# Causal attention: the probability-times-value products of two blocks issued together, every second block, with a third probability buffer

## The chip, the cores and the metric

One core of a Trainium2 chip runs the whole program in one launch. The metric is the time on the device in microseconds (us); lower is better. TensorE (PE in the profile) does the matrix products, VectorE (DVE) and ScalarE (ACT) work on their results in PSUM, GpSimd (POOL) does small preparations, SyncE (SP) issues most DMAs. Every engine works through its own list of instructions in order, and waits on semaphores for the others.

## What is computed

The reference is a small network on an input of 2 sequences x 1024 tokens x 128 channels: a feed-forward part, linear attention, the feed-forward part again, a mixture of 16 experts, causal attention, and the mixture again. Cut to what the change touches:

```python
x = x + 0.5 * _L1_ffn_ref(_layernorm(x), ...)        # experts
x = x + _L1_attn_ref(_layernorm(x), w_qkv, w_proj)   # causal attention, 16 heads of 8 channels
x = x + 0.5 * _L1_ffn_ref(_layernorm(x), ...)        # experts

# in _L1_attn_ref
att = jnp.einsum('bhtd,bhsd->bhts', q, k) * scale
att = jnp.where(causal, att, jnp.finfo(att.dtype).min)
att = jax.nn.softmax(att, axis=-1)
y = jnp.einsum('bhts,bhsd->bhtd', att, v)
```

All matrices are in 32-bit floats.

## The kernel before

The stages run one after the other: `ffn`, `linear`, `ffn`, `moe`, `causal`, `moe`. The change lies in `causal` alone.

`causal` works in 8 steps (STEPS): 2 sequences x 4 groups of 4 heads. A step has 12 blocks (NBLK, k = 0 to 11). Two kinds of work run side by side in it. For the step's own heads, a block of B_BLOCKS is one tile of 128 keys against up to 512 queries: the scores of one head are one matmul (`score`, L1595), on the diagonal a mask is added by two small matmuls (`mask`, L1607), ScalarE makes the probabilities exp(score) and writes them to a buffer `pb` in SBUF (L797), and TensorE multiplies them with the values (`sums`, L1552; the ninth column of the values is 1, so the softmax's denominator comes with it). The widths of the 12 blocks are 512, 384, 256, 128 for the first half of the queries, and 512 five times, 384, 256, 128 for the second. For the heads of the next step, a block of A_BLOCKS finds each query's largest score ahead of time: a matmul per head (`score_max`, L1629) and a reduction on VectorE (L1160 where a mask is added, L1163 where none is). Their widths are 512, 384, 256, 128, 512 five times, 384, 256, 128 too. The first round of the loop (step -1) has the largest scores alone, the last step (7) has none.

The matmuls of one head use 64 of the array's 128 rows, so a score and a largest-score matmul on different halves run side by side. A `sums` call has four heads, each with 9 output columns in a column group of its own, and the four run side by side; each takes two passes for 32-bit data, so the profile shows 8 matmuls.

The order on TensorE within a block is written out by hand:

```python
BLOCK_ORDER = (("score", 0), ("max", 0), ("max", 1), ("score", 1), ("mask", 0), ("mask", 1), ("score", 2),
               ("max", 2), ("mask", 2), ("sums", None), ("max", 3), ("score", 3), ("mask", 3))
```

`sums` in block k is that of block k-1. Below, "b6.max3" is the fourth largest-score matmul of block 6, the first one behind the place of `sums`.

Buffers: scores go through 3 PSUM banks (S_DEEP), largest scores through 3 others (A_DEEP). So a score matmul waits until the exponential of three scores earlier is done (`p_ready`), and a largest-score matmul until the reduction of three earlier is done (`a_free`). The sums of all heads are collected in one bank (bank 7), which ScalarE copies out after blocks 3 and 11 (`yraw`, L827). `pb` has two buffers, and the first exponential of block n waits for the sums of block n-2 (`pv_done`).

Behind each block stand hooks from a table (`schedule`): copies of the maxima into the queries (`maxima`, L1533 and L1535, behind blocks 1 and 5; VectorE prepares them in `negate` behind blocks 0 and 4), transposes of finished rows (`yout`, L1562, behind blocks 3 and 7; VectorE divides in the blocks after), and in some steps a projection, a layer norm and the routing of the next stage.

Of the kernel before, what the change touches and what calls it, by code (L numbers as in the profile page):

```python
# [22 lines left out]
ACT = mybir.ActivationFunctionType  # L23
AX = mybir.AxisListType

P = 128
# [4 lines left out]
CW = CT * P  # L31
# [9 lines left out]
G, GH = 4, 4  # L41
# [16 lines left out]
NBLK = len(B_BLOCKS)  # L58
# [6 lines left out]
STEPS = B * G  # L65
# [105 lines left out]
def macaron(nc, x_in, wa_in, wp_in, gw_in, uw_in, dw_in, q1_in, q2_in, small_in, rows_in, const_in, out):  # L171
    ctx = ExitStack()
    with ctx:
        def sb(name, shape, dt=F32):
            return ctx.enter_context(nc.sbuf_tensor(name, shape, dt))

        def sem(name):
            return ctx.enter_context(nc.semaphore(name))
# [74 lines left out]

        kza = sb("kza", [P, 4, 2, CW], F32R)
        gb = kt[:, G:G + 2, :].bitcast(F32).rearrange("p g (a n) -> p (g a) n", a=2)
        qtb = sb("qtb", [P, 2, S], F32R)
# [28 lines left out]
        pb = arena[:, 0:2 * GH * CW].rearrange("p (r h n) -> p r h n", r=2, h=GH)  # L287
# [50 lines left out]
        b_full, p_ready, pv_done = sem("b_full"), sem("p_ready"), sem("pv_done")  # L338
# [14 lines left out]
        def stg_done(n):  # L353

            if n < TB and n % 2:
                return stg_dve, n // 2 + 1
            return stg_pool, n // 2 + 1 if n < TB else TB // 2 + n - TB + 1

        def slot(b, g):

            return G * b + (g + 2) % G
# [14 lines left out]
        def s_bank(n):  # L376

            return bank[1 + n % S_DEEP]
# [222 lines left out]
        def _(act):  # L601
# [136 lines left out]
            def tiles(n, first=""):  # L738

                for todo in EARLY.get(("act" + first, n), []):  # L740
                    if todo[0] == "ln":
                        ln(todo[1])
                    if todo[0] == "qkv":
                        qkv_out(*todo[1:])
                    if todo[0] == "parts":
                        parts(*todo[1:])
                    if todo[0] == "alone":
                        alone(*todo[1:])

            def qkv_out(b, i):  # L750
                n = TB * b + i
                act.wait_ge(qkv_full, n + 1)
                if n % TB >= 2:
                    act.wait_ge(*stg_done(n - 2))
                    act.wait_ge(v_ready, n - 1)
                act.activation(qkv[b][:, n % 2, :], qkv_bank(b, i)[:, 0:3 * D], ACT.Copy).then_inc(qkv_ready, 1)

            def parts(b, i, which):
                n = 2 * (TB * b + i) + which
                act.wait_ge(kt_full, n + 1)  # L760
                act.activation((kt, qta)[which][:, G * b:G * (b + 1), i * P:(i + 1) * P],
                               keys_bank(b, i, which)[:, :].rearrange("p (g t) -> p g t", g=G), ACT.Copy)\
                    .then_inc(kt_ready, 1)

            def maxima(s, half):

                act.wait_ge(mx_full, 2 * s + half + 1)
                act.activation(qtb[:, s % 2, tok(half)], T[:, :], ACT.Copy).then_inc(qtb_ready, 1)
# [13 lines left out]
            def causal():  # L782
                for n in range(NC * NU, NC * NU + 4):
                    tiles(n, " first")
                    tiles(n)
                qkv_out(1, 0)
                for s in range(-1, STEPS):
                    for k, (c, j) in enumerate(B_BLOCKS):
                        if s >= 0:
                            blk = s * NBLK + k  # L790
                            w = min(CW, CW * (c + 1) - j * P)
                            for i, h in enumerate(S_HEADS):
                                n = blk * GH + i
                                act.wait_ge(b_full, n + 1)
                                if i == 0 and blk >= 2:
                                    act.wait_ge(pv_done, blk - 1)
                                act.activation(pb[:, blk % 2, h, 0:w], s_bank(n)[:, 0:w], ACT.Exp,  # L797
                                               scale=SCALE).then_inc(p_ready, 1)
                        for todo in HOOKS.get(("act", s, k), []):
                            if todo[0] == "ln":  # L800
                                ln(todo[1])
                            if todo[0] == "qkv":
                                qkv_out(*todo[1:])
                            if todo[0] == "parts":
                                parts(*todo[1:])
                            if todo[0] == "max":
                                maxima(*todo[1:])
                            if todo[0] == "yraw":
                                yraw(*todo[1:])
                            if todo[0] == "final":  # L810
                                final(*todo[1:])
                            if todo[0] == "alone":
                                alone(*todo[1:])
                            if todo[0] == "route":
                                route(4)
                            if todo[0] == "weights":
                                weights(4)
                yraw(STEPS - 1, 1)
                final(1, 1)
# [442 lines left out]
        def _(pe):  # L1262
# [159 lines left out]
            def weights(r):  # L1422
                pe.wait_ge(cw_ready, r + 1)
                t_take(cwt_ready, r + 1)
                for t in range(CT):
                    ins = pe.transpose(T[0:NR, t * P:(t + 1) * P], cw[:, t, :], ident[:, :])
                ins.then_inc(cw_full, 1)
# [110 lines left out]
            def sums(blk):  # L1538

                s, k = divmod(blk, NBLK)  # L1540
                c, j = B_BLOCKS[k]
                b, g = divmod(s, G)
                w = min(CW, CW * (c + 1) - j * P)
                pe.wait_ge(p_ready, GH * (blk + 1))
                pe.wait_ge(v_ready, TB * (b + 1))
                y = 2 * s + c
                if blk == 0:
                    pe.wait_ge(kt_ready, 2 * (TB + KEYS_ASIDE) - 1)
                if j == 0 and y >= 1:
                    pe.wait_ge(ysb_ready, y)  # L1550
                for h in range(GH):
                    ins = pe.matmul(bank[7][h * SL:h * SL + HD + 1, CW - w:CW], va[:, b, j, g * GH + h, :],  # L1552
                                    pb[:, blk % 2, h, 0:w], start=(j == 0), stop=True,
                                    skip_group_check=True)
                ins.then_inc(pv_done, 1)

# [24 lines left out]
            def causal():  # L1581
# [55 lines left out]
                for s in range(-1, STEPS):  # L1637
                    for k in range(NBLK):
                        now, ahead = s >= 0, s + 1 < STEPS
                        for kind, order in BLOCK_ORDER:  # L1640
                            if kind == "score" and now:
                                score(s, k, order)
                            if kind == "mask" and now:
                                mask(s, k, order)
                            if kind == "max" and ahead:
                                score_max(s + 1, k, order)
                            if kind == "sums" and now and s * NBLK + k >= 1:
                                sums(s * NBLK + k - 1)
                        for todo in HOOKS.get(("pe", s, k), []):
                            if todo[0] == "ln":  # L1650
                                ln(todo[1])
                            if todo[0] == "qkv":
                                make_qkv(*todo[1:])
                            if todo[0] == "parts":
                                parts(*todo[1:])
                            if todo[0] == "max":
                                maxima(*todo[1:])
                            if todo[0] == "yout":
                                yout(*todo[1:])
                            if todo[0] == "final":  # L1660
                                final(*todo[1:])
                            if todo[0] == "project":
                                project_out(*todo[1:])
                            if todo[0] == "route":
                                route(todo[1], 4)
                            if todo[0] == "weights":
                                weights(4)
                sums(STEPS * NBLK - 1)
                yout(STEPS - 1, 1)
                final(1, 1)  # L1670
# [79 lines left out]
```

## Time and profile before

| what | value |
|---|---|
| time, median of 3 runs | 695.76 us (692.46 to 700.74) |
| profiled execution: its time | 693.21 us |
| profiled execution: its span | 691.4 us |
| TensorE busy | 609.3 us (88%) |
| VectorE busy | 487.5 us (71%) |
| ScalarE busy | 346.6 us (50%) |
| GpSimd busy | 171.5 us (25%) |
| mean granted TensorE clock | 0.931 of full speed |
| the eight steps of `causal` | from about 303 to 582 us |

The span is the time from the first to the last instruction of the program in the trace; the execution's own time is 1.8 us more. Busy shares are means over stages with different limits, and matmuls are pipelined, so "busy" on TensorE also covers the time in which a result travels through the array.

### The profile page before, as it was taken

The page shows a single profiled execution, that of the slowest core. Times are in us where ns is not written, and L with a number is a line of the kernel's source. Part 1 is how long each engine was busy: PE and PEld are TensorE (multiplying, and loading weights), DVE is VectorE, ACT ScalarE, POOL GpSimd, SP SyncE. Part 2 cuts the span into 40 slices and gives each one's busy share as a digit, 9 for nine tenths or more (in the row PEclk, how much of TensorE's full clock was granted, in tenths as well). Part 3 has the DMA queues.
Part 4 walks back from the last instruction along what each step waited for, and adds up shares of the span by engine and source line. Part 5 has one row for each costly group of instructions (what it writes and reads, how often), then busy time and mean ns, then how long its engine had stood idle before and what let it go on. Part 6 is the DMA issues. An engine that isn't in the chain of part 4 may idle for free.

```text
span 691.4 us, 12355 instructions
## 1 busy us (share of the span) xinstructions
PE 609.3 (88%) x4284; PEld 424.0 (61%) x4284; DVE 487.5 (71%) x1526; ACT 346.6 (50%) x711; POOL 171.5 (25%) x304
## 2 busy tenths in 40 slices
PE   1876769769998987999999999998899997999997
PEld 1765657658887975665354444544444544888887
DVE  3558884558878775974678888879888521877765
ACT  3735236412233554565567777665677765232221
POOL 4565164432003363872111120203020000100000
PEclk9999879989999998865799999999999978999999
DMA  8000000022332210000000000000000001133342
GB/s 283 1 0 1 0 1 1 0 77 90 122 114 79 92 47 1 1 1 0 1 2 1 1 1 1 2 1 1 2 2 1 2 1 64 63 123 113 111 131 77
DMA packets 18669, 27.98 MB, mean 40 GB/s; under 512 B 2984, under 2 KB 7208, under 8 KB 18608
## 3 DMA queue, kind: packets, MB, share of 16 engines
q1 hardware_dynamic: 17888, 25.85, 11.7%
q10 hardware_dynamic: 720, 1.34, 0.6%
q8 instruction: 35, 0.57, 0.3%
q14 instruction: 26, 0.21, 0.1%
HBM read 25.85 MB, written 1.33 MB: 39 GB/s over the span
## 4 chain that ended last, share of the span: by engine, by line
PE 61%; DVE 17%; issue 5%; ACT 4%; POOL 3%; DMA 1%; SPq 0%; DVEq 0%; POOLq 0%
PE bank L1552 10%; PE bank L1483 9%; PE bank L1629 7%; PE bank L1595 7%; PE bank L1273 6%; PE bank L1275 6%; PE bank L1274 6%; DVE bank L1160 4%; DVE work L1163 3%; DVE hn L888 2%; ACT arena L797 2%; PE bank L1521 2%; PE bank L1533 1%; PE bank L1562 1%; PE bank L1607 1%
## 5 line engine op out<-in xcount | busy, mean ns | idle before, releaser
L797 ACT ACTIVATE arena<-bank 128x512 f32<-128x512 f32 (+3 forms) x384 | 166.4, 495 | 79.6 <-PE bank L1607 52.6
L1629 PE MATMUL bank<-kza,qta 64*128 64x512 f32 (+3 forms) x384 | 140.7, 443 | 9.4 <-DVE work L1160 5.1
L1160 DVE CUSTOM_DVE_ANT_0 bank<-bank,mask_qk 128x512 f32<-128x512 f32 (+3 forms) x256 | 119.1, 520 | 32.9 <-PE bank L1629 32.5
L1595 PE MATMUL bank<-qtb,kza 64*128 64x512 f32 (+3 forms) x384 | 137.3, 429 | 4.2 <-ACT arena L797 2.0
L1629 PEld LDWEIGHTS bank<-kza,qta 64*128 64x128 f32 x384 | 66.8, 201 | 86.9 <-DVE work L1160 46.6
L727 ACT ACTIVATE work<-bank 128x512 f32<-128x512 f32 x80 | 47.7, 597 | 117.6 <-PE bank L1275 112.3
L1163 DVE TENSOR_REDUCE work<-bank 128x1 f32<-128x512 f32 x128 | 80.4, 684 | 20.0 <-PE bank L1629 20.0
L1483 PE MATMUL bank<-dw,work 128*128 128x128 f32 x640 | 85.7, 278 | 6.0 <-DVE work L1090 6.0
L1483 PEld LDWEIGHTS bank<-dw,work 128*128 128x128 f32 x640 | 81.9, 193 | 10.1 <-issue 6.2
L1086 DVE TENSOR_TENSOR work<-work,bank 128x512 f32<-128x512 f32 x80 | 54.8, 685 | 47.0 <-PE bank L1275 41.3
L1552 PE MATMUL bank<-arena 128*9 128x512 f32 (+3 forms) x768 | 85.7, 520 | 0.4 <-ACT arena L797 0.4
L1595 PEld LDWEIGHTS bank<-qtb,kza 64*128 64x128 f32 x384 | 66.9, 196 | 31.4 <-ACT arena L797 18.2
L533 POOL CAST kza<-kt 32x512 fp32r<-32x512 f32 x48 | 29.2, 607 | 159.4 <-PE bank L1595 118.8
L455 POOL TENSOR_SCALAR rtmp<-mv 128x4 f32<-128x4 f32 x24 | 9.3, 387 | 220.8 <-DVE mv L876 220.6
L1090 DVE TENSOR_TENSOR work<-work,kt 128x512 f32<-128x512 f32 x80 | 56.3, 704 | 7.8 <-DMA kt<-cw_rows 5.1
L888 DVE TENSOR_SCALAR hn<-x,mv,rs 128x128 f32<-128x128 f32 x96 | 36.4, 444 | 19.9 <-POOL rs L472 16.2
L1607 PE MATMUL bank<-identb,mask_kq 64*128 64x64 bf16 x512 | 48.4, 199 | 0.0
L912 DVE SCALAR_TENSOR_TENSOR x<-bank,x 128x512 f32<-128x512 f32 x24 | 16.5, 689 | 31.0 <-PE bank L1577 13.3
L1273 PE MATMUL bank<-qta,gh 128*128 128x512 f32 x80 | 38.4, 480 | 0.0
L1281 PE MATMUL bank<-identr,hn 128*128 128x128 f32 x96 | 17.0, 305 | 24.0 <-DVE hn L888 24.0
L1313 PE MATMUL bank<-work 128*128 128x128 f32 x256 | 35.7, 287 | 2.0 <-ACT work L651 1.5
L1313 PEld LDWEIGHTS bank<-work 128*128 128x128 f32 x256 | 33.7, 200 | 6.0 <-DVE x L912 2.8
(179 smaller groups left out, 1083.9 us busy)
## 6 DMA issues: line engine op xcount, KB each, us to landing
kt<-cw_rows SPq DMA_DIRECT2D x160, 128.0 KB, 2.9
x<-x_in SPq DMA_DIRECT2D x4, 256.0 KB, 8.8
y_out<-x SPq DMA_DIRECT2D x4, 256.0 KB, 3.2
arena<-gw_in SPq DMA_DIRECT2D x1, 640.0 KB, 9.3
arena<-uw_in SPq DMA_DIRECT2D x1, 640.0 KB, 8.2
dw<-dw_in SPq DMA_DIRECT2D x1, 640.0 KB, 9.3
work<-q_in SPq DMA_DIRECT2D x2, 256.0 KB, 6.5
arena<-const_in ACTq DMA_DIRECT2D x1, 400.0 KB, 6.6
```

Source lines behind the costliest of these rows:

```text
L797: act.activation(pb[:, blk % 2, h, 0:w], s_bank(n)[:, 0:w], ACT.Exp, scale=SCALE).then_inc(p_ready, 1)
L1086: link(dve.tensor_tensor(su[:, m % 2, :], sg[:, m % 2, :], bank[4 + m % 3][:, :], ALU.mult))
L1090: dve.tensor_tensor(hbuf[:, m % 3, :], su[:, m % 2, :], gb[:, m % 4, :], ALU.mult)\
L1160: ins = dve.tensor_tensor_reduce(out=src, in0=src, in1=mask_qk[:, CW - w:], scale=1.0, scalar=-3e38, op0=ALU.add, op1=ALU.max, accum_out=dst)
L1163: ins = dve.tensor_reduce(dst, src, AX.X, ALU.max)
L1273: pe.matmul(dst, ah, bl, start=start, stop=False)
L1313: ins = pe.matmul(ACC[:, t * P:(t + 1) * P], hbuf[:, m % 4, t * P:(t + 1) * P], w2[:, k, :], start=(k == 0 and t == 0), stop=(k == FB - 1) ...
L1483: ins = pe.matmul(ACC[:, t * P:(t + 1) * P], hbuf[:, m % 3, t * P:(t + 1) * P], dw[:, u, :], start=(u == 0 and t == 0), stop=(u == NU - 1) ...
L1552: ins = pe.matmul(bank[7][h * SL:h * SL + HD + 1, CW - w:CW], va[:, b, j, g * GH + h, :], pb[:, blk % 2, h, 0:w], start=(j == 0), stop=Tru ...
L1595: ins = pe.matmul(s_bank(n)[:, 0:w], kz(s, h, j // CT)[pair(h), j % CT * P:(j % CT + 1) * P], qtb[pair(h), s % 2, (c + 1) * CW - w:(c + 1) ...
L1607: ins = pe.matmul(s_bank(n)[:, a * 2 * SL:(a + 1) * 2 * SL], mask_kq[r, a, :], identb[r, r], start=False, stop=True, skip_group_check=True)
L1629: pe.matmul(a_bank(n)[:, 0:w], qta[pair(h), slot(b, g), i * P:(i + 1) * P], kz(s, h, half)[pair(h), 0:w], start=True, stop=True).then_inc( ...
```

## The change

A third buffer of probabilities is added (`pb_last`, 8 KB per partition). Block n of the exponentials writes buffer n mod 3, and its first one waits for the sums of block n-3 in place of n-2. On TensorE the place of `sums` is used in even blocks alone, and there for two calls one behind the other, those of blocks k-2 and k-1. At the end, two calls remain in place of one. The number of matmuls, exponentials and reductions is the same.

```diff
+        pb_last = sb("pb_last", [P, GH, CW])
...
+        def probs(blk, h):
+
+            return pb[:, blk % 3, h, :] if blk % 3 < 2 else pb_last[:, h, :]
...
-                                if i == 0 and blk >= 2:
-                                    act.wait_ge(pv_done, blk - 1)
-                                act.activation(pb[:, blk % 2, h, 0:w], s_bank(n)[:, 0:w], ACT.Exp,
+                                if i == 0 and blk >= 3:
+                                    act.wait_ge(pv_done, blk - 2)
+                                act.activation(probs(blk, h)[:, 0:w], s_bank(n)[:, 0:w], ACT.Exp,
                                                scale=SCALE).then_inc(p_ready, 1)
...
                     ins = pe.matmul(bank[7][h * SL:h * SL + HD + 1, CW - w:CW], va[:, b, j, g * GH + h, :],
-                                    pb[:, blk % 2, h, 0:w], start=(j == 0), stop=True,
+                                    probs(blk, h)[:, 0:w], start=(j == 0), stop=True,
                                     skip_group_check=True)
...
-                            if kind == "sums" and now and s * NBLK + k >= 1:
+                            if kind == "sums" and now and k % 2 == 0 and s * NBLK + k >= 2:
+                                sums(s * NBLK + k - 2)
                                 sums(s * NBLK + k - 1)
...
+                sums(STEPS * NBLK - 2)
                 sums(STEPS * NBLK - 1)
```

## Rows read from the trace of the kernel before

**Rows 1.** The page: span, busy time of engines, chain by engine

```profile
span 691.4 us, 12355 instructions
PE 609.3 (88%) x4284; PEld 424.0 (61%) x4284; DVE 487.5 (71%) x1526; ACT 346.6 (50%) x711; POOL 171.5 (25%) x304
...
PE 61%; DVE 17%; issue 5%; ACT 4%; POOL 3%; DMA 1%; SPq 0%; DVEq 0%; POOLq 0%
```

**Rows 2.** Windows, steps 0, 2 and 7: length, busy time, clock

```profile
308.30:350.10 41.80, 39.06 (x263) 18.92 (x263) 23.03 (x74) 23.42 (x52) 6.60 (x14) 0.68 0.00 1
...
381.40:412.90 31.50, 29.97 (x278) 14.75 (x278) 26.75 (x89) 22.49 (x52) 4.86 (x8) 1.00 0.01 2
...
546.00:582.30 36.30, 34.09 (x261) 16.06 (x257) 6.49 (x36) 23.68 (x56) 0.00 (x0) 0.86 0.01 4
```

**Rows 3.** Chain, block 7 of step 2: start, us, what

```profile
400.43 0.61 ACT arena L797
```

**Rows 4.** Timeline of PE, block 7: start, us, instruction

```profile
399.86 0.50 PE L1629 MATMUL bank<-kza,qta 64*128 64x512 f32 x1
...
400.20 0.80 PE L1629 MATMUL bank<-kza,qta 64*128 64x512 f32 x2
400.51 1.07 PE L1595 MATMUL bank<-qtb,kza 64*128 64x512 f32 x2
401.14 0.50 PE L1629 MATMUL bank<-kza,qta 64*128 64x512 f32 x1
401.57 1.05 PE L1552 MATMUL bank<-arena 128*9 128x512 f32 x8
402.55 0.49 PE L1629 MATMUL bank<-kza,qta 64*128 64x512 f32 x1
```

**Rows 5.** Timeline of PE, 402.20 to 402.21: the second passes

```profile
402.01 0.61 PE L1552 MATMUL bank<-arena 128*9 128x512 f32 x4
```

**Rows 6.** Timeline of DVE, blocks 6 to 10

```profile
398.56 4.32 DVE L1163 TENSOR_REDUCE work<-bank 128x1 f32<-128x512 f32 x7 [0.63 <-PE bank L1629]
403.08 0.69 DVE L1163 TENSOR_REDUCE work<-bank 128x1 f32<-128x512 f32 x1 [0.20 <-PE bank L1629]
...
406.48 0.73 DVE L1160 CUSTOM_DVE_ANT_0 bank<-bank,mask_qk 128x512 f32<-128x512 f32 x1
...
407.13 0.60 DVE L1160 CUSTOM_DVE_ANT_0 bank<-bank,mask_qk 128x384 f32<-128x384 f32 x1
...
407.64 0.60 DVE L1160 CUSTOM_DVE_ANT_0 bank<-bank,mask_qk 128x384 f32<-128x384 f32 x1
```

**Rows 7.** Timeline of PE: max3 of blocks 0, 2, 4, 8, 10, 0

```profile
382.86 0.49 PE L1629 MATMUL bank<-kza,qta 64*128 64x512 f32 x1
...
388.97 0.38 PE L1629 MATMUL bank<-kza,qta 64*128 64x256 f32 x1
...
393.00 0.50 PE L1629 MATMUL bank<-kza,qta 64*128 64x512 f32 x1
...
405.66 0.50 PE L1629 MATMUL bank<-kza,qta 64*128 64x512 f32 x1
...
410.91 0.38 PE L1629 MATMUL bank<-kza,qta 64*128 64x256 f32 x1
...
414.32 0.49 PE L1629 MATMUL bank<-kza,qta 64*128 64x512 f32 x1
```

**Rows 8.** Timeline of PE, step 7, TensorE at half clock

```profile
562.79 1.90 PE L1552 MATMUL bank<-arena 128*9 128x512 f32 x8
564.62 1.22 PE L1595 MATMUL bank<-qtb,kza 64*128 64x512 f32 x3
...
566.82 1.89 PE L1552 MATMUL bank<-arena 128*9 128x512 f32 x8
```

**Rows 9.** Timeline of PE, the end of step 7

```profile
580.69 0.62 PE L1552 MATMUL bank<-arena 128*9 128x256 f32 x8
...
582.01 0.41 PE L1552 MATMUL bank<-arena 128*9 128x128 f32 x8 [0.37 <-ACT arena L797]
```

## The prediction

> **What bounds the kernel now.** I read the page first: a span of 691.4 us with TensorE busy for 88% of it, and 61% of the chain that ended last is TensorE, 17% VectorE, 4% ScalarE [rows 1]. That says TensorE matters most, but is a mean over stages. The change touches the causal stage alone, so next come the windows by step: step 2 takes 31.5 us with TensorE busy 30.0, VectorE 26.8, ScalarE 22.5; step 0 takes 41.8 (the profile's window starts a little inside it) at a mean granted clock of 0.68, the last 36.3 at 0.86 with almost nothing on VectorE [rows 2]. A busy TensorE is not a TensorE that computes: a 512-wide matmul stands in the record for 0.50 us, yet pairs follow each other after 0.31 to 0.34 (399.86, 400.20, 400.51) [rows 4]. So I went on to the order of starts in one full block, number 7 of step 2.
>
> From b6.max3 at 399.86 two pairs follow fast, then the third comes only at 401.08 and 401.14, where the others' pitch would put it at 400.84 [rows 4]. Two things end just before: the exponential of score 3, started at 400.43 and 0.61 long [rows 3], and the reduction of b6.max3, the fourth of the seven that start at 398.56 [rows 6]. Both hold a bank of a ring of three. This gives four terms:
> - L, from a matmul to the start of its reduction on an idle VectorE: 402.55 to 403.08, 0.53 [rows 4, 6].
> - P, VectorE's pitch: seven reductions in 4.32, the last 0.69 long, so (4.32 - 0.69) / 6 = 0.605 each [rows 6].
> - R, from a reduction's start to the matmul that takes its bank: the fourth starts at 398.56 + 3 x 0.605 = 400.38, the matmul at 401.14: 0.76, of which I take 0.74, since this matmul also follows the one of 401.08 by 0.06 [rows 4, 6].
> - from max2 to the sums 0.43 (401.14 to 401.57), the sums themselves 0.98 (401.57 to 402.55) [rows 4].
>
> L + R + 0.43 + 0.98 = 2.68, and the block takes 2.69 (399.86 to 402.55). So a full block is set by a loop: the matmul behind the sums, its reduction, the return of the bank, the matmul ahead of the sums, the sums. VectorE needs 4 x 0.605 = 2.42 in it and is idle for the rest, since nothing new reaches it while the sums run (0.63 and 0.20 before two of its rows) [rows 6]. TensorE alone would need four pairs at about 0.32 and the sums with their entry, 2.4 too. Three engines' limits lie within 15% of each other.
>
> **What the change removes.** The sums' two passes start 0.44 apart (401.57, 402.01) [rows 4, 5]; the next kind of matmul starts 0.98 - 2 x 0.44 = 0.10 later than a further pass would. Going in, 0.43 against a pair's 0.31 to 0.34 is another 0.10 [rows 4]. The Trainium skill says why this may be (TensorEngine Tiling (Array Packing), Key Properties): a change between tiling modes drains the array; the rows agree, with 0.10 at either side. Before there are 96 calls in 96 places; after, 47 places with two and one pair at the end, so 48 round trips of 0.20 to 0.23 go: 9.6 to 11.0 us, if TensorE set every block. At half clock a call takes 1.83 (562.79 to 564.62), its passes about twice as long and its exits too [rows 8].
>
> **What it adds.** The sums come as one stretch of 4 x 0.434 + 0.10 = 1.85 in place of two of 0.98, and VectorE and ScalarE still have only three banks each. In the odd block nothing is between the pairs, so they run at VectorE's pitch. The full walk for b6.max3 to b8.max3, which the trace has as 399.86 to 405.66, 5.80 [rows 4, 7]: the reduction of b6.max3 starts at 0.53, the four of block 7 at P each, the last at 0.53 + 4 x 0.605 = 2.95; its bank comes back at 2.95 + 0.74 = 3.69, which lets b8.max2 go; the mask's matmuls and the entry take 0.47, the sums of blocks 6 and 7 1.85: 6.01. TensorE's own way there (the output transposes behind block 7 included) would be some 0.15 shorter, so they lie beneath VectorE's work, and this is 0.2 slower than before in spite of a round trip less.
>
> The other pairs by the same rules. Passes go by width, so calls of 512, 384, 256 and 128 columns take 0.98, 0.76, 0.54 and 0.32, and doubles 0.10 less than their sum [rows 4, 5]. VectorE's pitch with a mask is 0.65 at 512 and 0.51 at 384 (406.48, 407.13, 407.64) [rows 6]; I take 0.38 and 0.25 for 256 and 128 by the same step, R 0.81, 0.67, 0.55, 0.40 and L 0.53, 0.47, 0.42, 0.36, estimates from the 512 terms with a step of a width's share. Before, from the starts of max3 [rows 4, 7]; after, by the chain that ends last:
> - b0 to b2: before 6.11. After: b0.max3's reduction starts at 0.59, behind its forerunner; 0.65 later the negate, about 0.52, so block 1's first reduction at 1.76; + 0.67 gives max3 at 2.43. From there to block 2's first pair TensorE copies the maxima, 1.33 as before; two more pairs 0.41, entry 0.36, double of 512 and 384 1.64: 6.17.
> - b2 to b4: before 4.03. After: score 2 of block 3 at 0.93, when ScalarE gives its bank back, as before; max3 at 0.77 + 0.40 = 1.17; to block 4's first pair 0.91 with the output transposes, as before; pairs 0.58, entry 0.32, double of 256 and 128 0.79: 3.77.
> - b4 to b6: before 6.86. After: the divide (0.5) is still in VectorE's queue, so b4.max3's reduction starts at 1.19; 0.60 and the negate's 0.31 later that of b5.max0, 2.10; + 0.74 gives b5.max3 at 2.84; copies 1.30, pairs 0.58, entry 0.33, double 1.85: 6.90.
> - b6 to b8: 5.80, after 6.01.
> - b8 to b10: before 5.25. After, by VectorE alone: 0.53 + 0.65 + 3 x 0.515 + 0.67 = 3.40, entry 0.33, double of 512 and 384 1.64: 5.37.
> - b10 to the next b0: before 3.41. After: reductions start at 0.42, 0.77, 1.02, 1.33 and 1.58; + 0.40 gives the bank back at 1.98 and block 0's third pair at 2.05; entry 0.45, double of 256 and 128 0.77: 3.27.
>
> Sum: before 31.46 (382.86 to 414.32), after 31.49. The step does not change: 6 x 0.2 of round trips are gained and as much is lost to VectorE's hunger in the doubles. I take +0.03 +- 0.5 for each of steps 1 to 6: +0.2, between -3 and +3.
>
> Step 0 is at half clock for most of its length, where VectorE has time to spare, and carries the second sequence's transposes too: four of its six pairs give 0.3 each and the rest nothing, -0.9 (bounds 0 and -2). Step 7 has no largest scores; full blocks there close their loop through ScalarE and cost 0.14 more a pair at full clock, while at half clock (4.03 a block, 562.79 to 566.82) [rows 8] a round trip of 0.3 to 0.4 comes through; with the hooks, and with a sums call gone from ahead of the last score, I take -0.8 (bounds +0.5 and -2). The end adds a call of 256 columns, 0.54, but TensorE waits 0.37 there for the last exponential, and score 3 comes 0.6 earlier without the call at 580.69 [rows 9]: nothing.
>
> Edits that cost nothing: the third buffer; block n's first exponential now waits for sums that TensorE has done a block before, and even in the kernel before the wait was for work issued ahead of the score that it reads. `yraw` waits for the sums of blocks 3 and 11, which stay in blocks 4 and 0; the next first call on bank 7 moves a block later, so TensorE waits for that copy less. GpSimd's copies are gated by scores two steps back. Moved past: the copies and transposes of the hooks now stand ahead of the sums of their odd block; nobody waits for those sums but `yraw`. If the cover of the hooks (VectorE's queue) is gone, they cost their 0.6 to 0.9 each.
>
> **Sum.** +0.2 - 0.9 - 0.8 = -1.5 on the profiled 693.21: 691.7. That execution was 2.5 below the median 695.76, so as a median 694.3. What these measurements can tell from no change is about 1% (7 us).
>
> **Rivals.**
> 1. The round trips come through in full, because VectorE catches up elsewhere. For it: TensorE holds 61% of the chain [rows 1], busy 30.0 of 31.5 [rows 2]. Against: the loop of 2.68 with its wait at 401.08. It gives 48 x 0.22 = -10.6: 685.2. Chance 0.19.
> 2. Slower: the double starves VectorE and ScalarE and the hooks no longer lie beneath VectorE's work. Place: b6.max3 to b8.max3, where I found only 0.15 between the two ways. Then 0.6 of transposes come on top of 6.01, and as much or more in b4 to b6 and b8 to b10: +1.6 a step, over 7 steps +11, less 1.5: 705. It decides when TensorE, coming out of a double, is later with its third pair than VectorE's return of the bank. Chance 0.13.
> 3. The clock. It is 1.00 in step 2 [rows 2], with sums spread over each block. The odd block and the pairs after it are now a stretch of 3.7 us or more with light matmuls alone. If that brings the clock down to its lower level of 1.2 GHz, full blocks go towards 4.0 [rows 8]; one such stretch of about 1.4 us lost in each of seven steps is +10: 703. Against: the narrow blocks 2 and 3 are light in every step, and the clock stays at 1.00. Chance 0.07. The Trainium skill has such a rule (TensorE: Matmul & The Clock Gate, A second HAM failure mode: psum-queue depth-cycling): a TensorE that idles shortly between groups of matmuls can swing between its clocks; no row here shows it within steps 1 to 6.
> 4. The dense double brings the clock up sooner in step 0 (0.68) or 7 (0.86) [rows 2]: 4 to 8 us less, 688. Chance 0.07.
> That the third buffer does nothing by itself is part of my forecast: no exponential waited for the sums.
>
> **Chances and range.** The forecast, 690 to 699, has 0.54. The range 685 to 701 takes in most of rival 4, about half of rival 1 and the near part of 2 and 3. Faster by over 1%: most of rival 1 and half of 4, 0.22. Slower by over 1%: 2 and 3 mostly, 0.17. Between: 0.61.
>
> **What would show it.** In the trace after: sums as x16 of about 1.9 us every second block; b6.max3 to b8.max3 6.0 in step 2 with VectorE idle for about 1.1 in front of one reduction; the step 31.5. A step of 30.3 would mean rival 1, one of 33 rival 2, a clock below 1.00 in steps 1 to 6 rival 3. I am wrong if TensorE's pairs in the odd block don't slow to 0.6 apart, or if the wait behind the double is not VectorE's.

## The result and the profile after

| | before | changed |
|---|---|---|
| median of 20 runs each | 696.31 us (687.49 to 708.98) | 701.78 us (695.53 to 714.09) |
| ratio, 95% interval | | 1.0104 (1.0073 to 1.0135) |
| span of the profiled execution | 691.4 us | 698.6 us |
| its mean granted clock | 0.931 | 0.916 |

The change makes the kernel 1% slower; forecast was 694.3, no change. The ratios here leave out runs over 1.5% above the fastest of their kernel, and since TensorE's clock varies from run to run in this kernel and sets most of that spread, this takes out more runs of one kernel than of another (of the kernel before 16 of the 29 beside e1 to e4, 10 of the 17 beside e5 to e8, 4 of the 17 beside e9 to e12), so medians over all runs stand beside them.

The page after, its lines that answer to [rows 1]:

```profile
span 698.6 us, 12354 instructions
PE 609.0 (87%) x4284; PEld 437.0 (63%) x4284; DVE 484.4 (69%) x1526; ACT 345.4 (49%) x711; POOL 171.4 (25%) x304
...
PE 61%; DVE 18%; issue 4%; ACT 4%; POOL 3%; DMA 1%; SPq 0%; DVEq 0%; POOLq 0%; ACTq 0%
```

Nothing shows there: the same work, 7 us more span. The windows by step do show it (length; busy time and number of instructions of PE, PEld, DVE, ACT, POOL; granted clock; DMA share; GB/s). After, steps 2 to 6:

```profile
380.40:412.00 31.60, 29.00 (x280) 16.03 (x275) 26.47 (x92) 22.47 (x53) 4.86 (x8) 1.00 0.01 2
412.00:446.20 34.20, 31.88 (x288) 17.80 (x287) 26.66 (x90) 23.05 (x54) 4.86 (x8) 0.95 0.01 2
446.20:485.50 39.30, 33.68 (x289) 18.01 (x288) 30.63 (x113) 23.22 (x53) 6.54 (x12) 0.91 0.00 1
485.50:525.60 40.10, 36.27 (x277) 18.77 (x274) 27.50 (x94) 22.45 (x52) 5.71 (x9) 0.79 0.00 1
525.60:557.00 31.40, 28.78 (x278) 15.80 (x273) 26.26 (x90) 22.27 (x53) 2.43 (x4) 1.00 0.00 1
```

Before, steps 3 to 6 of the same list (step 2 is in [rows 2]):

```profile
413.00:445.60 32.60, 31.58 (x290) 15.96 (x287) 27.12 (x88) 22.99 (x53) 4.87 (x8) 1.00 0.01 2
445.60:481.70 36.10, 32.48 (x291) 16.43 (x290) 30.45 (x113) 23.17 (x53) 6.52 (x12) 1.00 0.00 1
481.70:514.20 32.50, 30.01 (x277) 14.70 (x276) 28.16 (x95) 22.50 (x52) 5.73 (x9) 1.00 0.01 2
514.20:545.60 31.40, 29.88 (x277) 14.65 (x276) 26.75 (x89) 22.48 (x52) 2.43 (x4) 1.00 0.01 1
```

Where the clock is 1.00, in steps 2 and 6, the step is as long as before. Steps 3, 4 and 5 lost 1.6, 3.2 and 7.6 us, and there the clock is 0.95, 0.91 and 0.79. Those shares mean 1.7, 3.5 and 8.4 us more than at full clock, (1 - clock) x length, as a fall to half doubles what TensorE takes: all of the loss, and a little more. Steps 0 and 7 went the other way in this pair of executions (46.4 to 42.3, 35.6 to 34.0), with their clocks (0.67 to 0.78, 0.86 to 0.95). Step -1 is 2.1 longer (31.0 to 33.1) with its clock at 0.50 in place of 0.72. So one pair of executions holds several differences of the clock, and only the runs as a whole say which of them belong to the change.

Cut finer, each of the five falls (to the lower level, 1.2 GHz) comes behind a stretch in which TensorE had no sums: four of them behind block 1 or 5, the one at 485.7 where step 4 goes over into step 5. Windows of after, the stretch and the fall behind it, three of five:

```profile
414.00:417.40 3.40, 2.83 (x25) 1.99 (x23) 3.33 (x14) 3.05 (x7) 0.74 (x2) 1.00 0.02 5
417.40:420.80 3.40, 3.40 (x25) 1.46 (x28) 1.58 (x8) 1.53 (x4) 0.00 (x0) 0.50 0.00 0
...
489.10:492.50 3.40, 1.62 (x19) 1.17 (x17) 3.08 (x12) 2.23 (x5) 0.00 (x0) 1.00 0.00 0
492.50:499.30 6.80, 6.80 (x43) 3.33 (x42) 2.45 (x12) 2.02 (x5) 0.00 (x0) 0.50 0.01 4
502.70:506.10 3.40, 2.39 (x19) 1.14 (x11) 3.33 (x10) 3.08 (x7) 0.00 (x0) 1.00 0.01 2
506.10:513.00 6.90, 6.90 (x31) 2.62 (x31) 3.15 (x6) 2.77 (x5) 0.00 (x0) 0.51 0.00 0
```

TensorE's timeline before the first of them shows what is in such a stretch, block 1 of step 3:

```profile
414.59 0.44 PE L1600 MATMUL bank<-qtb,kza 64*128 64x384 f32 x1
...
415.23 0.44 PE L1634 MATMUL bank<-kza,qta 64*128 64x384 f32 x1
...
416.24 0.44 PE L1634 MATMUL bank<-kza,qta 64*128 64x384 f32 x1 [0.56 <-DVE work L1165]
...
416.69 0.66 PE L1538 MATMUL bank<-identr,stm 128*128 128x128 f32 x4
417.19 0.56 PE L1540 MATMUL bank<-qta,identr 128*128 128x512 f32 x1
```

A few pairs on half the rows, a wait of 0.56 for VectorE, four transposes: the work between two doubles is thin because the doubles took the dense part out of it. The waits ahead of the other falls are as long or longer: 0.59 and 0.41 before those at 461.8 and 506.1, 1.02 before 485.7 and 1.60 before 492.5, all for VectorE. Step 1 has the same stretch without sums in block 1, with the same wait of 0.56 (ahead of the pair at 353.20), and the clock holds there: the stretch makes a fall possible, not certain.

At full clock the walk of the prediction holds. Starts of max3 in step 2, and VectorE's rows for the double that ends at 399.12:

```profile
399.12 0.50 PE L1634 MATMUL bank<-kza,qta 64*128 64x512 f32 x1
```

```profile
395.54 3.30 DVE L1168 TENSOR_REDUCE work<-bank 128x1 f32<-128x512 f32 x5
399.66 3.08 DVE L1168 TENSOR_REDUCE work<-bank 128x1 f32<-128x512 f32 x5 [0.83 <-PE bank L1634]
```

VectorE idles 0.83 before one reduction (0.20 and 0.63 in [rows 6]; the prediction's sign was about 1.1), and then has five in a row.

| stretch | before | forecast | after (step 2) |
|---|---|---|---|
| b0 to b2 | 6.11 | 6.17 | 6.17 (382.27 to 388.44) |
| b2 to b4 | 4.03 | 3.77 | 3.80 |
| b4 to b6 | 6.86 | 6.90 | 6.88 |
| b6 to b8 | 5.80 | 6.01 | 5.95 (to 405.07) |
| b8 to b10 | 5.25 | 5.37 | 5.34 |
| b10 to b0 | 3.41 | 3.27 | 3.39 (to 413.80) |
| step | 31.46 | 31.49 | 31.53 |

### The profile page after: what moved, and what is told of

Same layout as the page of the kernel before. It is cut to its first block, busy times and chain, and to the rows that moved or that the text cites. A ratio compares the mean times of both kernels' runs of the same rounds, so it can differ in the third digit from the quotient of the medians.

```text
span 698.6 us, 12354 instructions
## 1 busy us (share of the span) xinstructions
PE 609.0 (87%) x4284; PEld 437.0 (63%) x4284; DVE 484.4 (69%) x1526; ACT 345.4 (49%) x711; POOL 171.4 (25%) x304
## 4 chain that ended last, share of the span: by engine, by line
PE 61%; DVE 18%; issue 4%; ACT 4%; POOL 3%; DMA 1%; SPq 0%; DVEq 0%; POOLq 0%; ACTq 0%
PE bank L1557 10%; PE bank L1488 9%; PE bank L1634 8%; PE bank L1278 6%; PE bank L1280 6%; PE bank L1600 6%; PE bank L1279 6%; DVE bank L1165 5%; DVE work L1168 4%; DVE hn L893 2%; PE bank L1526 2%; PE bank L1538 2%; PE bank L1567 1%; PE bank L1286 1%; PE bank L1612 1%
## 5 line engine op out<-in xcount | busy, mean ns | idle before, releaser
L1634 PE MATMUL bank<-kza,qta 64*128 64x512 f32 (+3 forms) x384 | 138.5, 458 | 15.1 <-DVE work L1168 6.7
L1165 DVE CUSTOM_DVE_ANT_0 bank<-bank,mask_qk 128x512 f32<-128x512 f32 (+3 forms) x256 | 118.4, 519 | 40.8 <-PE bank L1634 40.2
L1600 PE MATMUL bank<-qtb,kza 64*128 64x512 f32 (+3 forms) x384 | 134.3, 422 | 6.8 <-ACT arena L802 2.8
L802 ACT ACTIVATE arena<-bank 128x512 f32<-128x512 f32 (+3 forms) x256 | 113.7, 508 | 47.4 <-PE bank L1612 22.4
L1634 PEld LDWEIGHTS bank<-kza,qta 64*128 64x128 f32 x384 | 68.2, 208 | 63.8 <-issue 20.2
L802 ACT ACTIVATE pb_last<-bank 128x512 f32<-128x512 f32 (+2 forms) x128 | 52.9, 469 | 38.2 <-PE bank L1612 35.1
L1557 PE MATMUL bank<-arena 128*9 128x512 f32 (+3 forms) x512 | 58.9, 559 | 0.0
```

The source lines that it names most:

```text
L802: act.activation(probs(blk, h)[:, 0:w], s_bank(n)[:, 0:w], ACT.Exp, scale=SCALE).then_inc(p_ready, 1)
L1165: ins = dve.tensor_tensor_reduce(out=src, in0=src, in1=mask_qk[:, CW - w:], scale=1.0, scalar=-3e38, op0=ALU.add, op1=ALU.max, accum_out=dst)
L1600: ins = pe.matmul(s_bank(n)[:, 0:w], kz(s, h, j // CT)[pair(h), j % CT * P:(j % CT + 1) * P], qtb[pair(h), s % 2, (c + 1) * CW - w:(c + 1) ...
L1634: pe.matmul(a_bank(n)[:, 0:w], qta[pair(h), slot(b, g), i * P:(i + 1) * P], kz(s, h, half)[pair(h), 0:w], start=True, stop=True).then_inc( ...
```

## The experiments

Two theories went in: the clock falls in the light stretches that doubles leave (rival 3, the clock theory), or VectorE and ScalarE go hungry in the doubles (rival 2, the hunger theory). "Clock" below is the mean granted clock over all runs of a kernel; the kernel before has 0.920 (63 runs), the changed one 0.912 (20 runs). "Half clock" is the time at the lower level within steps 1 to 6, in us, of the one profiled execution. "Step" is step 1 or 2 where it ran at full clock.

| run | ratio | medians, this / before | clock | half clock | step |
|---|---|---|---|---|---|
| before | | | 0.920 | 0 | 31.5 |
| changed | 1.0104 (1.0073 to 1.0135) | 701.8 / 696.3 = 1.008 | 0.912 | 27 | 31.5 |
| e1 single sums, third buffer | 1.0009 (0.996 to 1.0058) | 693.1 / 695.7 = 0.996 | 0.922 | 10 | 31.5 |
| e2 changed, filler in all odd blocks | 1.0097 (1.0057 to 1.0137) | 701.7 / 695.7 = 1.009 | 0.926 | 10 | 32.2 |
| e3 doubles in steps 3 to 5 | none | 707.2 / 695.7 = 1.017 | 0.915 | 20 | 31.5 |
| e4 doubles outside 3 to 5 | 0.9985 (0.9941 to 1.003) | 696.7 / 695.7 = 1.001 | 0.927 | 17 | 31.5 |
| e5 doubles in blocks 0, 4 | 0.9881 (0.9795 to 0.9966) | 684.2 / 697.7 = 0.981 | 0.930 | 3 | 30.4 |
| e6 doubles in blocks 2, 6 | 1.0298 (1.0228 to 1.0368) | 711.6 / 697.7 = 1.020 | 0.908 | 41 | 32.4 |
| e7 changed, filler in blocks 1, 5 | 1.0102 (1.0023 to 1.0181) | 698.4 / 697.7 = 1.001 | 0.926 | 17 | 31.9 |
| e8 before, filler in steps -1, 0 | 1.0012 (0.9959 to 1.0066) | 695.1 / 697.7 = 0.996 | 0.947 | 10 | 31.5 |
| e9 doubles in blocks 8, 10 | 1.0023 (0.9983 to 1.0063) | 696.5 / 695.9 = 1.001 | 0.920 | 14 | 31.7 |
| e10 = e6 with dense filler in 1, 5 | 1.0142 (1.0085 to 1.0198) | 704.8 / 695.9 = 1.013 | 0.929 | 3 | 33.2 |
| e11 = e5 again | 0.980 (0.9746 to 0.9853) | 679.6 / 695.9 = 0.977 | 0.939 | 0 | 30.4 |
| e12 = e5, filler in step -1 | 0.9702 (0.9644 to 0.9759) | 673.7 / 695.9 = 0.968 | 0.961 | 3 | 30.4 |

The 0 of the kernel before belongs to its one profiled execution. e1 and e8 have its order in steps 1 to 6, and 10 us at half clock there.

**e1: the third buffer without doubles.**

```diff
-                            if kind == "sums" and now and k % 2 == 0 and s * NBLK + k >= 2:
-                                sums(s * NBLK + k - 2)
+                            if kind == "sums" and now and s * NBLK + k >= 1:
                                 sums(s * NBLK + k - 1)
...
-                sums(STEPS * NBLK - 2)
                 sums(STEPS * NBLK - 1)
```

> The changed kernel with the order on TensorE put back: one sums call in every block, while the third buffer of probabilities and the later wait stay. Both theories (the clock falls in the light stretches that the doubles leave; or VectorE and ScalarE go hungry in the doubles) expect the time of the kernel before within 0.5%, about 694 to 699 us, the clock at 1.00 in steps 1 to 6, and steps 1, 2 and 6 at 31.5 us. If the buffer's place in SBUF or the other wait mattered, it would be as slow as the changed kernel, 1% more.

As both expected in time: no cost of the buffer and the wait shows, within 0.6%. The clock at 1.00 in steps 1 to 6 did not come: the profiled execution had a poor clock (0.905), with one fall in step 3 and one in step 4, both in the middle of single sums. The order before isn't free of falls, and a stretch without sums isn't the only place for one; what speaks for fewer falls is the mean clock over the runs (0.920 and 0.922 against 0.912).

**e2: every score of the odd blocks twice.**

```diff
-                    ins = pe.matmul(s_bank(n)[:, 0:w], ...
+                    for again in range(2 if k % 2 and s + 1 < STEPS else 1):
+                        ins = pe.matmul(s_bank(n)[:, 0:w], ...
```

> The changed kernel, but in odd blocks of steps 0 to 6 every score matmul is issued twice (the second writes the same values over the first), so that the stretch without sums holds more matmuls; no wait and no other engine's work changes. Clock theory: the odd blocks have room on TensorE (VectorE paces them), so steps 1, 2 and 6 stay at 31.5 to 32.3 us, the falls of the clock in steps 3 to 5 go away or get fewer (mean clock 0.93 or more in place of 0.916), and the time comes down to that of the kernel before or some us below, ratio 0.985 to 1.003. Hunger theory: more work on TensorE can't help; the time stays at ratio 1.01 or gets worse by up to 0.2 us for each of 42 odd blocks, 1.01 to 1.02.

A miss by the numbers: 0.93 or more and at most 1.003 were expected, 0.926 and 1.0097 came, and 1.01 was the hunger theory's number. The direction is the clock theory's: the mean clock rose from 0.912 to 0.926, the profile has two falls in place of five in steps 1 to 6, and the filler cost 0.7 us a step and ate the gain (b6 to b8 went from 5.95 to 6.08, b4 to b6 to 7.12). The time alone tells nothing here.

**e3 and e4: doubles in some steps.** The calls not yet made are kept in a counter; a place of sums makes all that are due.

```diff
-                            if kind == "sums" and now and k % 2 == 0 and s * NBLK + k >= 2:
-                                sums(s * NBLK + k - 2)
-                                sums(s * NBLK + k - 1)
+                            if kind == "sums" and now and not (s in (3, 4, 5) and k % 2):
+                                while summed[0] < s * NBLK + k:
+                                    sums(summed[0])
+                                    summed[0] += 1
```

> Doubles in steps 3, 4 and 5 alone (those with extra hooks, where the changed kernel's profile has its low clock), single sums elsewhere. Clock theory: all of the loss is here, ratio 1.008 to 1.02, low clock only in steps 3 to 5 (and where the kernel before has it). Hunger theory: the loss is spread over the steps, so about 3 of 7 of it, ratio 1.004.

> Doubles in all steps but 3, 4 and 5. Clock theory: steps 1, 2 and 6 keep their 31.5 us at full clock, step 0 and 7 gain a little, ratio 0.990 to 1.000. Hunger theory: about 4 of 7 of the loss, ratio 1.006.

e3's six runs fall apart, two at 688.7 and 694.5 (clocks 0.943, 0.931) and four at 706.6 to 710.1 (0.901 to 0.910), so no ratio came out; time and clock go together in that spread. By medians e3 is 1.017, inside the clock theory's 1.008 to 1.02, and its profile has all of its low clock of steps 1 to 6 in steps 4 and 5. e4 came out level, inside the clock theory's 0.990 to 1.000, but not for the reason expected. In its profile the clock falls in step 2 and step 6, two plain steps:

```profile
378.20:411.30 33.10, 30.52 (x277) 16.30 (x275) 26.37 (x91) 22.47 (x53) 4.88 (x8) 0.95 0.01 1
...
512.60:550.10 37.50, 34.69 (x269) 17.59 (x265) 26.20 (x88) 22.21 (x52) 2.44 (x4) 0.82 0.00 1
```

So falls do not need the extra hooks of steps 3 to 5. All three falls again come behind block 1 or 5. That led to the next question: which doubles?

**e5, e6 and e9: which pairs of blocks.** e5 skips the place of sums in blocks 3 and 11 (doubles in 4 and 0), e6 in blocks 1 and 5 (doubles in 2 and 6), e9 in 7 and 9 (doubles in 8 and 10).

```diff
-                            if kind == "sums" and now and not (s in (3, 4, 5) and k % 2):
+                            if kind == "sums" and now and k not in (3, 11):
```

> Doubles in blocks 0 and 4 alone (the sums of blocks 10 and 11, and of 2 and 3), single sums in all others. Between two places of sums there are then at most about 3 us. Clock theory, as it stands after the first four runs: falls follow the long stretches without sums (block 0 to 2 and 4 to 6, 4.5 to 5 us in the changed kernel), so the low-clock time is that of the kernel before, and the steps at full clock are 0.2 us shorter (31.25): ratio 0.993 to 1.002. Hunger theory, and a theory that any double brings the clock down: a third of the loss stays, ratio 1.003 or more.

> Doubles in blocks 2 and 6 alone (sums of 0 and 1, and of 4 and 5), single sums in all others. Their trace at full clock should be that of the kernel before within 0.1 us a step (31.5), since both pairs of blocks took 6.15 and 6.89 before and after. Clock theory: most of the loss is here, low-clock time up by 8 us or more over the runs, ratio 1.005 to 1.012. Hunger theory: no loss, ratio 1.000 to 1.002.

> Doubles in blocks 8 and 10 alone (sums of 6 and 7, of 8 and 9), single sums elsewhere. In the changed kernel b6.max3 to b8.max3 took 5.94 in place of 5.80 and b8 to b10 5.34 in place of 5.25, so both theories expect a step at full clock to be 0.2 to 0.4 us longer than 31.47, 1.5 to 3 us in all. The stretches between sums are about 4 us. If falls of the clock need the copies of the maxima in the stretch (4.5 us and more), few are added and the ratio is 1.002 to 1.006; if 4 us without sums is enough, low-clock time is up by 8 us or more and the ratio above 1.008.

> Doubles in blocks 0 and 4 alone, a second time, for the number: ratio 0.983 to 0.992, a step at full clock 30.43 us.

The three kernels part the change into thirds, and it comes apart into a gain and a loss: -1.2 and -2.0% (two sets of runs), +3.0%, +0.2% by the ratios, -1.9 and -2.3, +2.0, +0.1% by the medians. The forecasts of the size missed for e5 (0.993 to 1.002), e6 (1.005 to 1.012) and just so for e11 (0.983 to 0.992), the first and the last by more gain, e6 by more loss; e9's (1.002 to 1.006) held. Two things are in it. At full clock a step takes 30.4, 32.4 and 31.7 us against 31.5: -1.0, +0.9, +0.2, together +0.1, where the changed kernel, with all three, has +0.06. I had expected e6 level and e5 at 31.25; both were further out. Step 2 of e5 and of e6:

```profile
376.20:406.60 30.40, 29.09 (x277) 15.00 (x274) 26.49 (x90) 22.58 (x53) 4.88 (x8) 1.00 0.01 2
```

```profile
388.80:421.20 32.40, 29.71 (x280) 15.07 (x279) 26.80 (x89) 22.48 (x52) 4.86 (x8) 1.00 0.01 2
```

In e5, b0 to b2 takes 5.67 (before 6.11), b2 to b4 3.80 (4.03), b4 to b6 6.51 (6.86): behind a double of narrow blocks VectorE comes to the negate 1.23 behind b0.max3 (before 1.70) and to the divide 0.12 behind b4.max3 (0.46), and the blocks behind, which wait for it, gain as well. In e6, b0 to b2 takes 6.63 and b4 to b6 7.24, and the negate comes 1.71 behind b0.max3.

And the clock: 0.930 and 0.939 in the two runs of e5, 0.908 in e6, 0.920 in e9. Step 1 of e6, whole, then a stretch and the fall behind it:

```profile
351.80:388.80 37.00, 34.32 (x279) 16.26 (x279) 26.80 (x89) 22.59 (x52) 4.86 (x8) 0.86 0.01 1
354.80:358.20 3.40, 2.83 (x31) 1.92 (x30) 3.07 (x14) 2.66 (x7) 0.00 (x0) 1.00 0.00 0
358.20:361.60 3.40, 3.40 (x21) 0.74 (x19) 0.91 (x6) 0.77 (x3) 0.00 (x0) 0.50 0.03 5
```

The same step takes 37.0 in place of 32.4. In e6's profile all seven falls of steps 1 to 6 come behind block 1 or block 5. e9 had three falls, in steps 2 and 4, one of them behind a block 5 with single sums and two in block 10, and its mean clock is that of before.

**e7 and e10: filler in those blocks.** e7 is the changed kernel with every score of blocks 1 and 5 twice. e10 is e6 with three scores and two largest-score matmuls in place of one there.

```diff
-                    ins = pe.matmul(s_bank(n)[:, 0:w], ...
+                    for again in range(3 if k in (1, 5) and s + 1 < STEPS else 1):
+                        ins = pe.matmul(s_bank(n)[:, 0:w], ...
...
-                    pe.matmul(a_bank(n)[:, 0:w], ...
+                    for again in range(2 if k in (1, 5) and s > 0 else 1):
+                        ins = pe.matmul(a_bank(n)[:, 0:w], ...
```

> The changed kernel, with every score matmul issued twice in blocks 1 and 5 of steps 0 to 6 alone. Before, with the filler in all odd blocks, the mean clock rose from 0.912 to 0.926, but a step at full clock took 32.2 in place of 31.5 us. Clock theory: most of that rise with half of the cost: clock 0.92 or more, step 31.8, ratio 0.998 to 1.006. Hunger theory: 1.010 or more.

> The kernel with doubles in blocks 2 and 6 (ratio 1.030), with every score matmul of blocks 1 and 5 issued three times and every largest-score matmul twice, steps 0 to 6; no wait changes. Clock theory: the stretches that were light are dense now, the mean clock rises from 0.908 to 0.925 or more, no falls behind blocks 1 and 5; a step at full clock gets 0.5 to 1.5 us longer than its 32.4; ratio 1.015 to 1.030, that is not slower than without the filler, in spite of about 10% more matmuls. If the clock does not go by what TensorE does there, the clock stays at 0.908 and the ratio is 1.035 or more.

e7 was within its clock (0.926), its step came at 31.9 (31.8 expected), and its ratio of 1.0102 is outside the 0.998 to 1.006 of the clock theory, while its medians give 1.001: from e7 alone no gain over the changed kernel can be told. e10 settles the cause. It only adds matmuls, its step at full clock is 0.8 longer than e6's, and yet it is faster: 704.8 against 711.6, every run of e10 (701.0 to 709.2) below every run of e6 (710.1 to 719.6). The kernel before was 1.8 us faster beside e10's runs than beside e6's, which leaves 4.9 of the 6.7 us; the ratios, 1.030 and 1.014, say more. Step 1 of e10, then steps 1 to 6 together, e10 and e6:

```profile
349.50:382.70 33.20, 31.60 (x300) 16.87 (x301) 26.80 (x89) 22.61 (x52) 4.86 (x8) 1.00 0.01 1
349.50:556.10 206.60, 194.57 (x1816) 104.72 (x1817) 166.08 (x560) 136.87 (x314) 29.27 (x48) 0.99 0.01 2
```

```profile
351.80:570.80 219.00, 200.30 (x1670) 99.54 (x1669) 166.27 (x560) 136.76 (x314) 29.26 (x48) 0.91 0.00 1
```

The mean clock went from 0.908 to 0.929, and one short fall is left in steps 1 to 6 where e6 had seven: 144 matmuls more in these six steps, and in this pair of executions 12.4 us less. The hunger theory has no way to make a kernel faster by more work on its busiest engine. What e10 does not part: the filler is both more work and shorter idle time on TensorE, so whether the thin matmuls or the waits between them bring the falls is not shown.

**e8 and e12: filler ahead of step 0.** e8 is the kernel before with the largest-score matmuls of step -1 three times and the scores of step 0 twice; e12 is e5 with the first of these alone.

```diff
-                    pe.matmul(a_bank(n)[:, 0:w], ...
+                    for again in range(3 if s == 0 else 1):
+                        ins = pe.matmul(a_bank(n)[:, 0:w], ...
```

> The kernel before, unchanged in its order; in step -1 every largest-score matmul is issued three times, in step 0 every score matmul twice (no effect on values). In the kernel before, TensorE is at half clock for 24 us of step 0. If denser matmuls bring the clock up, step 0 gets 3 to 8 us shorter: ratio 0.990 to 0.996. If the clock in that stretch does not go by what TensorE does, the ratio is 1.000 to 1.010, for the work added.

> As the run before it, and in step -1, where TensorE waits for others, every largest-score matmul is issued three times (no effect on values), to have the clock up when step 0 begins. If that holds, mean clock 0.94 or more and 3 to 6 us less than without: ratio 0.977 to 0.987. If the clock falls again in step 0, or the filler costs what it gains, the same as without, 0.988 or a little more.

e8 missed: its clock is the highest of any with the old order (0.947) and step 0 got shorter in its profile (40.4), but over the runs it is level. Its trace shows where the gain went in that execution: it is 7.1 us ahead of the kernel before at the first score of step 1, loses 4.3 of them in steps 3 and 4, each with a fall (35.8 and 37.1 us against 32.7 and 35.9), and 4.2 in step 7 (41.0 against 36.8 to the end of the last sums, with 20 us at half clock against 10). e12, which fills only where TensorE waits for others, is the fastest: 0.9702, 673.7 us, better than the 0.977 to 0.987 expected. Its runs (670.3 to 682.8) overlap those of e11 (678.1 to 685.2), with five of its six below all of e11's. Steps -1, 0 and 1 in it, then step -1 and 0 of e11:

```profile
272.70:302.80 30.10, 29.69 (x212) 23.25 (x212) 27.05 (x88) 15.15 (x27) 23.97 (x52) 0.93 0.00 1
302.80:338.50 35.70, 31.91 (x284) 17.35 (x284) 26.55 (x87) 27.05 (x60) 11.85 (x26) 1.00 0.01 1
338.50:368.90 30.40, 29.09 (x276) 15.00 (x276) 26.51 (x91) 22.60 (x53) 4.84 (x9) 1.00 0.01 2
```

```profile
272.00:306.00 34.00, 33.58 (x121) 21.74 (x120) 27.82 (x88) 16.11 (x29) 25.25 (x55) 0.50 0.00 0
306.00:348.00 42.00, 38.79 (x290) 21.03 (x290) 27.07 (x88) 27.38 (x59) 11.20 (x24) 0.78 0.01 1
```

Step -1 goes from 34.0 to 30.1 us, step 0 from 42.0 to 35.7, with its clock from 0.78 to 1.00.

## Why the prediction was wrong, step by step

- **The loop, the terms, the walk: right.** With round trips of 0.20, the loop of 2.69 and VectorE's hunger in wide doubles the walk gave 31.49 a step; measured at full clock: 31.53. No forecast of a single stretch is off by more than 0.12, and the errors partly cancel. Three slips in it changed nothing that it rests on. 4 x 0.434 + 0.10 is 1.84 and not 1.85. "Three engines' limits lie within 15%" holds for TensorE and VectorE alone: ScalarE's exponentials start 0.48 apart (three from 398.59 on take 1.57 us, the last of them about 0.61), 1.9 a block. And rival 3's 703 adds its 10 us to the profiled time; on the forecast of 694.3 it is 704.
- **Rival 1** (round trips in full) is refuted for this change by the steps at full clock. That the third buffer does nothing by itself was right (e1).
- **The likeliest case left out the clock: the step that failed.** The sum holds no term for the clock in steps 1 to 6; it was put at 1.00 there, after as before. The runs showed falls in its place: 27 us at half clock in steps 3 to 5 of the profile, which cost 12.4 us there, and a median 5.5 us higher over the runs. The prediction's own sign for rival 3, a clock below 1.00 in steps 1 to 6, is what came. I gave rival 3 a chance of 0.07 and set against it that "the narrow blocks 2 and 3 are light in every step, and the clock stays at 1.00". The narrow blocks of the kernel before have sums in between. What set them apart is that in the changed kernel the sums stay away through the whole of blocks 1 and 5, with the copies of the maxima and waits for VectorE besides. I had worked those very stretches out and priced them at full clock. That doubles in these blocks bring the falls is shown by e6, e5 and e10; that it is the thin work in them, and not the waits, is argued. The rule named there (the Trainium skill, TensorE: Matmul & The Clock Gate, A second HAM failure mode: psum-queue depth-cycling) says that short idles of TensorE between groups of matmuls can make its clock swing between the two levels. The windows of after agree, with five swings to half behind waits of 0.41 to 1.60 us. Rival 3's own price, about 1.4 us for one fall in each of seven steps, was close to the profile by luck (+10 against the 12 us of steps 3 to 5; over the runs it is 5.5) and wrong in shape: no fall in steps 1, 2 and 6, five in steps 3 to 5.
- **Rival 2** did not come in the changed kernel (31.53 a step, not 33). The prediction had a gain and a loss of 1.2 us a step in balance, round trips against hunger, and in size that is right. What it did not see is that they lie in different blocks and can be had apart: the wide doubles of 2 and 6 alone lose 0.9 a step (e6), the narrow ones of 0 and 4 alone gain 1.0 (e5).
- **Steps 0 and 7:** forecast -0.9 and -0.8, profile -4.1 and -1.6, with the clock of those stretches. Step 0 took 43.4 us in e1, with single sums, and 40.2 in e9, at clocks of 0.75 and 0.86, so this isn't the doubles' doing. The two terms can't be read out of profiles in which the clock moves by more than they are worth, and it stays open whether they were right.
- **How much is the clock.** Within one kernel the runs spread over clock: the changed one from 695.5 us at 0.924 to 714.1 at 0.895, 18.6 us for 0.029, a little over 6 us for 0.01 between these ends; a straight line through all its runs gives 4.7 us for 0.01, one through the 63 of the kernel before 4.5. The means differ by 0.008: some 4 of the 5.5 us. The mean clock doesn't carry the rest, probably because of where the falls lie: in a step that TensorE sets, half clock costs half of its length, in step -1 less (e11 to e12: 0.50 to 0.93, 3.9 us of 34.0).

## What to carry to other kernels

Gathering the dense matmuls of a loop also makes the stretch between them light; ask what is left on TensorE there, and for how long, before counting what the gathering saves. A change that is level as a whole may be a gain and a loss: cut it by place. Here doubles of the narrow blocks alone gave 1 to 2% (e5, e11), and with cheap repeats of matmuls where TensorE waits anyway 3% (673.7 us), where the whole change lost 1%. A profile is one execution: the kernel before had no fall in steps 1 to 6 in its own, and two in each of the other two profiles with its order.

## What the runs showed of the hardware

TensorE's granted clock fell in the middle of a loop whose TensorE was busy for over 90% of the time by the record (31.88 of 34.20 us), without any wait above 0.6 us in the row ahead of the first fall; the busy time of a whole step does not tell whether the clock will hold. In the rows just ahead of the falls shown it was busy for 2.83, 1.62 and 2.39 of 3.40 us. In steps with the same work within one execution the clock falls in some and not in others (e6: step 1 at 0.86 and 37.0 us, step 2 at 1.00 and 32.4). It also differs between executions of one kernel, and the time with it (changed kernel: 695.5 us at 0.924, 714.1 at 0.895). More work on the engine can buy time: e10 against e6 (704.8, 711.6), e12 against e11 (673.7, 679.6).
